# Values of the windowed attention layers projected once per token and carried through DRAM

## What is computed

```python
qkv = x @ Wqkv
q, k, v = jnp.split(qkv, 3, -1)
...
def look(t):
    p = jnp.pad(t, ((0, 0), (0, 0), (1, 0), (0, 0), (0, 0)))
    return jnp.concatenate([p[:, :, :nw], p[:, :, 1:]], axis=3)
bk2, bv2 = (look(bk), look(bv))
...
sim = jnp.einsum('bhwie,bhwje->bhwij', bq, bk2) * QK_SCALE
...
attn = jax.nn.softmax(sim, -1)
out = jnp.einsum('bhwij,bhwje->bhwie', attn, bv2)
```

## Time and profile before

| | us |
|---|---|
| median of 3 runs (7240.41 to 7246.15) | 7244.83 |
| the profiled execution | 7247.5 |
| its span | 7245.8 |
| the loop of the local layers, from 2273 to 6280 | 4007 |
| one iteration of it, of 95 alike | 42.11 |

### The profile page before, as it was taken

One profiled execution on the slowest core, in us unless ns is written; L12 is line 12 of the kernel. 1 busy time (PEld: TensorE's weight loads), 2 busy tenths in 40 slices (PEclk: granted clock), 3 DMA queues, 4 the chain that ended last, 5 costly groups with the idle time before them and its releaser, 6 DMA issues. The chain is left out here.

```text
span 7245.8 us, 217809 instructions
## 1 busy us (share of the span) xinstructions
PE 6522.4 (90%) x79314; PEld 4468.9 (62%) x79314; DVE 4927.7 (68%) x14182; ACT 4182.4 (58%) x10030; POOL 2901.3 (40%) x2911
## 2 busy tenths in 40 slices
PE   7999979999988888888888888888888888879998
PEld 5777657776655565555555556555555555557676
DVE  4555535555657777777777777777777777668378
ACT  4666637776224655656655665565665566446355
POOL 0000010000004666666666666666666666530030
PEclk9999989999989999999999999999999999979999
DMA  1000000000000000000000000000000000010210
GB/s 34 24 25 25 23 27 29 28 28 22 10 33 20 23 4 5 23 4 5 5 23 5 4 5 22 5 5 4 23 5 4 23 4 5 5 37 16 81 38 24
DMA packets 131939, 133.17 MB, mean 18 GB/s; under 512 B 40302, under 2 KB 121982, under 8 KB 130814
## 3 DMA queue, kind: packets, MB, share of 16 engines
q1 hardware_dynamic: 115454, 103.45, 4.4%
q0 software_dynamic: 7936, 24.28, 1.1%
q10 hardware_dynamic: 8448, 4.20, 0.2%
HBM read 55.48 MB, written 10.49 MB: 9 GB/s over the span
## 5 line engine op out<-in xcount | busy, mean ns | idle before, releaser
L937 POOL TENSOR_TENSOR l_rot<-l_rot,l_by_sin 128x512 f32<-128x512 f32 x768 | 961.1, 1272 | 438.6 <-DVE l_by_sin L1301 424.5
L944 POOL TENSOR_TENSOR l_rot<-l_rot,l_norms 128x512 f32<-128x512 f32 x768 | 793.7, 1064 | 485.0 <-DVE l_norms L1322 485.0
L1019 PE MATMUL bank<-w_w,l_x 128*128 (+1 forms) x1536 | 802.0, 631 | 133.8 <-DVE l_by_sin L1301 126.3
L1198 ACT ACTIVATE l_squares<-bank 128x512 f32<-128x512 f32 x768 | 447.5, 596 | 518.9 <-DVE l_square_sums L1306 491.8
L1025 PE MATMUL bank<-w_w,l_x_windows 128*128 (+1 forms) x1536 | 721.0, 602 | 0.0
L1297 DVE TENSOR_TENSOR l_rot<-bank,l_cos 128x512 f32<-128x512 f32 x768 | 519.2, 676 | 295.7 <-ACT l_squares L1198 294.4
L486 PE MATMUL bank<-a_qk 64*128 64x256 f32 (+2 forms) x2660 | 679.5, 381 | 6.1 <-DVE a_qk L668 3.5
L402 POOL DMA_DIRECT2D a_w<-in_a x23 | 13.0, 565 | 1554.2 <-PE bank L514 1431.0
L593 ACT ACTIVATE a_probs_t<-bank 128x512 f32<-128x512 f32 (+1 forms) x656 | 355.9, 554 | 353.7 <-PE bank L494 353.7
L1219 ACT ACTIVATE l_probs_t<-bank 128x512 f32<-128x512 f32 x384 | 208.7, 595 | 598.2 <-PE bank L1061 598.2
L1035 PE MATMUL bank<-ident,l_rot 128*128 128x128 f32 x3072 | 476.4, 283 | 74.3 <-ACT l_probs_t L1219 48.0
(11 more groups left out here) (265 smaller groups left out, 14415.8 us busy)
## 6 DMA issues: line engine op xcount, KB each, us to landing
a_x<-normed_t SPq DMA_DIRECT2D x320, 128.0 KB, 2.0
l_stage_rows<-inner SPq DMA_DIRECT2D x98, 128.0 KB, 2.1
w_w<-in_w SPq DMA_DIRECT2D x6, 2048.0 KB, 9.5
l_shifted_half<-inner SPq DMA_DIRECT2D x98, 63.5 KB
f_w<-in_f SPq DMA_DIRECT2D x9, 514.5 KB, 3.2
a_w<-in_a POOLq DMA_DIRECT2D x18, 256.0 KB, 2.9
f_w<-in_f POOLq DMA_DIRECT2D x9, 512.0 KB, 4.4
c_x<-normed_t SPq DMA_DIRECT2D x36, 128.0 KB, 2.0
```

The costliest lines, as they stand in the source:

```text
L937: nc.gpsimd.tensor_tensor(rot[s][n][:], rot[s][n][:], by_sin[n % 2][:], ALU.add).then_inc(summed, 1)
L944: nc.gpsimd.tensor_tensor(mine, mine, along(norms[s][:, 8 * n:8 * n + 8], HD), ALU.mult)\
L1019: nc.tensor.matmul(rows_p[i][:], x[:, W + i * P:W + (i + 1) * P], layer_w(layer, quad * QUAD, QUAD), start=True, stop=True).then_inc(rows_ ...
L1198: nc.scalar.activation(squares[i][:], rows_p[i][:], ACT.Square).then_inc(squared, 1)
```

## The change

The values are projected once per token. `project_v` multiplies the two tiles of 128 tokens of x by the same 512 columns of weights: two matmuls in a half in place of four. ACT moves both banks into `v_rows` [128, 2, 512], ahead of the first exponential. SP then stores `v_rows` (512 KB) to a DRAM buffer `values` of 288 rows by 512, one buffer for each o, whose first 32 rows are zero; and reads it back with four DMAs of 256 KB, each for 32 partitions of `v`, rows of 2 KB: 128 rows of the buffer from 0, 32, 128 and 160 on, so that each token lands both as "own" and as "before". `weigh` waits for these reads (`v_loaded`), the read waits until `weigh` of unit h is through with the old values (`heads_filled`), and ACT waits before it fills `v_rows` that the store before has landed (`v_stored`).

The values are now of unit h + 2 (before: h + 1), so they are projected in both halves behind `project_rows`, ahead of `output` in the first half. POOL's copy and `x_windows` are gone, and ACT no longer moves values between or behind the exponentials. `gates`, `output` and the transposes keep their places. The load of `w_f` at a layer's fourth iteration stands behind the store and the reads of the first half; scales and `w_w` behind those of the second.

```diff
-                def copy_window(f):
-                    pool.wait_ge(x_moved, f + 1)
...
                 def project_v(o, fill, layer):
-                    for j in range(4):
-                        reached(pe, t_freed[j % 2], fill + j // 2)
-                        nc.tensor.matmul(t_p[j % 2][:], x_windows[:, j].rearrange("p t s c -> p (t s c)"),
-                                         layer_w(layer, wv_at + o * QUAD, QUAD), start=True, stop=True)\
-                            .then_inc(t_filled[j % 2], 2)
+                    for i in range(2):
+                        reached(pe, t_freed[i], fill)
+                        nc.tensor.matmul(t_p[i][:], x[:, tile_of(i)], layer_w(layer, wv_at + o * QUAD, QUAD), start=True,
+                                         stop=True).then_inc(t_filled[i], 2)
...
+                def store_v(u, o, fill):
+                    for i in range(2):
+                        sp.wait_ge(t_freed[i], fill + 1)
+                        sp.sem_inc(begun, 1)
+                    sp.dma_start(v_dram[o][W:, :].rearrange("(i p) n -> p i n", p=P), v_rows[:]).then_inc(v_stored, DMA)
+
+                def load_v(u, o):
+                    sp.wait_ge(v_stored, (u + 1) * DMA)
+                    sp.sem_inc(begun, 1)
+                    for i in range(2):
+                        for s in range(2):
+                            at = i * P + s * W
+                            sp.dma_start(v[HD * i + W * s:HD * i + W * (s + 1), :, o * QUAD:(o + 1) * QUAD],
+                                         v_dram[o][at:at + P, :].rearrange("(j c) n -> c j n", c=W)).then_inc(v_loaded[o], DMA)
...
+                def send_v(g, o):
+
+                    h = 2 * g + o
+                    sp.wait_ge(v_loaded[o], (g + 1) * 4 * DMA)
+                    sp.sem_inc(begun, 1)
+                    store_v(h + 2, o, t_fill(h))
+                    sp.wait_ge(heads_filled, 4 * h + 4)
+                    sp.sem_inc(begun, 1)
+                    load_v(h + 2, o)
...
                     for e in range(2):
                         pe.wait_ge(t_freed[e], fill + 1)
                     pe.wait_ge(masked, 2 * h + 2)
+                    pe.wait_ge(v_loaded[o], ((h >> 1) + 1) * 4 * DMA)
...
+                def move_v(u, i, fill):
+                    act.wait_ge(t_filled[i], 2 * (fill + 1))
+                    if i == 0:
+                        reached(act, v_stored, u * DMA)
+                    nc.scalar.activation(v_rows[:, i, :], t_p[i][:], ACT.Copy).then_inc(t_freed[i], 1)
...
                         exps(h, 0)
-                        if more:
-                            move_v(1 - o, 2, fill)
                         exps(h, 1)
-                        if more:
-                            move_v(1 - o, 3, fill)
                         if o == 1 and not last:
                             move_x(g + 2, f_fill(g) + 1)
```

More of the change, by code:

```diff
@@ L816, in local_layers @@
         stage_rows = sb("stage_rows", [P, 2, D])
-        x, x_windows = sb("x", [P, W + SEQ]), sb("x_windows", [P, 4, 2, 2, W])
+        x, v_rows = sb("x", [P, SEQ]), sb("v_rows", [P, 2, QUAD])
+        v_dram = [nc.dram_tensor(f"{name}_values{o}", (W + SEQ, QUAD), F32, kind="Internal").ap() for o in range(2)]
         scales, tables = sb("scales", [P, 2, QUAD]), [sb(n, [P, 2, QUAD]) for n in ("cos", "sin")]
@@ L845, in t_fill @@
         def t_fill(h):
-            return 5 * h + 4
+            return 4 * h + 4 if not isinstance(h, int) or h <= 2 * LAST else 8 * LAST + 7
         def f_fill(g):
@@ L894, in iteration @@
                     stage_x(g + 2)
+                    if not last:
+                        send_v(g, 0)
                     sp.wait_ge(normed, g + 1)
@@ L899, in iteration @@
                     shift((g + NB - 1) & (NB - 1))
+                    if L is not None:
+                        sp.wait_ge(ffn_added, NB * L + 19)
+                        sp.sem_inc(begun, 1)
+                        sp.dma_start(fw[:], t["f2"][bass.ds(L + 1, 1), :, :].rearrange("a p n -> p (a n)"))\
+                            .then_inc(fw_loaded, DMA)
+                    if not last:
+                        send_v(g, 1)
+                def send_v(g, o):
[4 more added lines that the diff above has]
+                    sp.wait_ge(heads_filled, 4 * h + 4)
+                    sp.sem_inc(begun, 1)
+                    load_v(h + 2, o)
                 def load_layer(L):
-                    sp.wait_ge(ffn_added, NB * L + 19)
-                    sp.sem_inc(begun, 1)
-                    sp.dma_start(fw[:], t["f2"][bass.ds(L + 1, 1), :, :].rearrange("a p n -> p (a n)")).then_inc(fw_loaded, DMA)
                     sp.wait_ge(tables_ready, L + 1)
@@ L912, in load_layer, with layer @@
                         .then_inc(w_loaded, DMA)
+                def layer(L):
+                    with sp.Fori(0, 2) as m:
+                        iteration(NB * L + m)
+                    iteration(NB * L + 2, L)
+                    load_layer(L)
                 load_scales(0)
                 stage_x(0)
+                sp.wait_ge(cleared, 2)
+                for o in range(2):
+                    sp.dma_start(v_dram[o][0:W, :], heads_t[0:W, 0:2, :].rearrange("p a n -> p (a n)")).then_inc(v_cleared, DMA)
+                sp.wait_ge(v_cleared, 2 * DMA)
                 shift(NB - 2)
@@ L918, in _ @@
                 stage_x(1)
[L919 to L922, removed]
+                for u in range(2):
+                    store_v(u, u, u)
+                    load_v(u, u)
+                with sp.Fori(0, DEPTH - 1) as L:
+                    layer(L)
                     with sp.Fori(3, NB) as m:
                         iteration(NB * L + m)
+                layer(DEPTH - 1)
+                with sp.Fori(NB * (DEPTH - 1) + 3, LAST) as g:
+                    iteration(g)
+                iteration(LAST, last=True)
                 sp.wait_ge(normed, LAST + 2)
@@ L1144, in iteration @@
                         fill, more = t_fill(h), o == 0 or not last
-                        turned = fill + 2 if more else fill
+                        turned = fill if last else fill + 1
                         if not last:
@@ L1165, in iteration @@
                         if more:
-                            turn_qk(h + 1, 1 - o, fill + 3)
+                            turn_qk(h + 1, 1 - o, turned + 1)
                         if o == 0:
@@ L1248, in start @@
                     square(0, 1)
-                    for j in range(4):
-                        move_v(0, j, 0)
+                    for i in range(2):
+                        move_v(0, i, 0)
                     square(1, 0)
                     square(1, 1)
+                    for i in range(2):
+                        move_v(1, i, 1)
                     move_qk(0, 2)
```

53 lines of the change are left out of this document (18 added, 35 removed).

## The result

| | us |
|---|---|
| before, median of 15 runs (7237.98 to 7246.15) | 7242.86 |
| after, median of 15 runs (7242.49 to 7267.86) | 7256.37 |
| ratio, with its 95% interval | 1.0019 (1.0011 to 1.0027) |
| profiled execution of after, its span | 7253.68, 7252.0 |

The account below looks back on a forecast made before the run. Waits for DVE, not PE, were taken to pace most of the first half, and ACT's move of x `gates`. Terms -116 + 4 + 2 + 29 = -81 us gave 7164 us, range 7110 to 7250.

Parts of the forecast that it names:

- The chain: Waits through one loop iteration, with PE's work removed: 40.89 us against 42.11, 1.22 saved, 116 us over 95 iterations.
- the rival that PE is the bound: Waits for DVE close up and all 3.59 us an iteration arrive: 6904 us; whole or half gain 7%.
- only the first part of the gain comes: Second half's gain is eaten by an unseen wait; 0.74 us by 95 remains: 7210 us; 10%.
- the clock: Longer idle ahead of `gates` (3.11 us) lowers PE's clock in one iteration in five: 19 falls at 1.54 us, 29 us.
- The first rival: Clock falls in most iterations at the idle between `turn_x` and `gates`: up to 7281 us, slower; 14%.
- Layer boundaries: `w_f`, queued behind four reads on SP, reaches `gates` about 0.4 us late at five boundaries: 2 us, up to 15.
- Transfers: Two stores and eight reads more on SP in each iteration slow the engines by 0.04 us: 4 us.
- the rival of late transfers: A store taking over 20 us delays ACT's moves, exponentials and DVE; at 21 us, 7354 us; 6%.
- the idles of `turn_normed`: Sign on PE: `turn_normed` idles 1.1 us, ended by `normalise_rows`; `gates` idles about 3.1 us.
- the quiet `weigh`: Sign on PE: `weigh` waits for no DMA, the reads being issued some 38 us earlier.
- the undisturbed period: Sign in the loop: the period between two `stage_x` falls to 40.9 us, or 41.2 in the mean.
- the loop's clock: Sign in the loop: clock below 1.00 by a few hundredths; below 0.93, falls in most iterations are at work.

Follow-up runs that it names:

- the doses above: Kernel after with one or two matmuls on constants in PE's idle ahead of `gates`: 7205.58 and 7159.89 us; with four, 7152.96.
- no_transfers: Kernel after without the store of `v_rows`, the reads back into `v` and their waits (`v` is zeros): 7286.01 us, ratio 1.0065.
- fill_second: Kernel after plus four matmuls on constants (about 1.9 us) between `turn_x` and `gates` in every second half: 7152.96 us, ratio 0.9877.
- before_short: Kernel before, with second-half `project_v` matmuls on 320 of 512 columns, so a longer idle ahead of `gates`: 7305.49 us, ratio 1.0082.
- fill_first: Kernel after plus four matmuls on constants (1.9 us) in the first half, ahead of `output`: 7345.89 us, ratio 1.0144.
- wf_early: Kernel after with the load of `w_f` issued ahead of SP's four reads at a layer's fourth iteration: 7246.81 us, ratio 1.0008.

## Why the prediction was wrong

**The chain was right**, step by step: start to the end of `normalise_rows` 17.90 (18.00 forecast), to PE 0.14 (0.20), `turn_normed` to `weigh` 0.38 (0.31), to DVE's rotation 3.87 (3.87), to the second exponential 7.46 (7.46), to `gates` 1.39 (1.39), to the end 9.65 (9.66). Sum 40.79 against 40.89. That only a third of PE's 3.59 us arrives, and that the second half's 1.88 merely lengthen the idle, is what the trace shows; the rival that PE is the bound (6904) is out, and so is that only the first part of the gain comes.

**The term that failed is the clock.** The prediction named the place and the mechanism, and then chose one iteration in five, 19 falls at 1.54 us, 29 us. It was 57 of 93, and the falls away from the boundaries cost 2.0 us each (100 us for 51); with the boundaries' share some 112 us. Both factors were low: the step put at 29 us cost four times that. The count rested on two idles of the earlier trace rows, 2.39 with a fall and 2.57 without; the second stands in another stage, with other work around it. In this loop the doses above give the count that was missing: an idle of 2.3 cost 7 falls, one of 2.75 26, one of 3.19 51. Whether the other idles of the iteration (0.84 us at `ups`, 1.3 at `project_rows`) set that tolerance was not tested. Choosing near the low end because the rows show "idle alone deciding nothing" used the openness of the evidence as if it were evidence for few. The price rested on a single fall that hit `project_rows`, a group of 1.98 us; behind `gates` it hits four groups in a row, all on the chain.

The first rival had the right mechanism, and its break-even of 75% of the iterations at 1.54 us becomes 59% at the measured price (1.16 / 1.96, the 1.96 from 112 / 57). The real share, 57 of 93 or 61%, is just past it, so the gain and the loss nearly cancel. The rule cited from the Trainium skill, TensorE: Matmul & The Clock Gate, "HAM oscillation — how this bites in real kernels", that each wait costs the clock of the burst behind it, was nearer than my number, though 36 of the 93 iterations kept it. The section tells it of waits for DMA that are longer than the idle here, a condition that the prediction left out.

**Layer boundaries** were put at 2 us, 15 at most, and took 19 beside their clock. There are six and not five, and the 15 has no working: reads of 11.6 us, put into the sum beside it, would make `w_f` 9.2 us late at each. The order on SP was read rightly, the four reads were overpriced (1.73 for all, against 2.8), but the step kept the `shift` between the reads and `w_f` at its time of before: its second DMA held SP for 5.15 us in place of 2.59. It is the new transfers ahead of it that do this: the median over the loop is 2.63 before, 5.04 in after and 2.68 in no_transfers. `w_f` was issued 29.25 us after the iteration's start (3067.01 - 3037.76, where its `project_rows` begins), not 27.7. In fill_second a late `w_f` cost 5.1 us a boundary, since it cost a fall too.

**Transfers.** The 4 us were some 13: 0.14 an iteration, against 0.04 taken from the boundary of before. Both new waits stay hidden, as forecast; the store of 512 KB lands in 3.2 us and a read of 256 KB in 4.4, within the bounds given, and the rival of late transfers is out:

```profile
l_v<-l_values SPq DMA_DIRECT2D x768, 256.0 KB, 4.4
l_values<-l_v_rows SPq DMA_DIRECT2D x192, 512.0 KB, 3.2
```

**Of what was to be seen**, the idles of `turn_normed` (0.79, 1.1 forecast) and `gates`, the quiet `weigh` and the undisturbed period came true; the mean period was 42.2, not 41.2, and the loop's clock 0.96, not below the 0.93 that I had set for the first rival, though that rival was at work. That mark was set too low: the second of the four iterations above lost 1.7 us and still shows 0.96.

## What to carry to other kernels

When an edit takes work from PE in a stretch that ends in a wait for another engine, it doesn't shorten the stretch but lengthens the rest, and the rest can cost the clock of what follows it: read the gain from the chain of waits, and then price the new idle by what stands behind it on PE, not by a fall seen elsewhere. If the count of falls is unknown, a run with a little useless work in the idle tells what they cost, and may be the remedy as well. Real work freed from its wait, here by another PSUM bank for `turn_x`, shortens the chain, but in this kernel it kept the clock only together with the useless work (7142 us alone, 7126 with the useless work alone, 7084 with both). A DMA queued ahead of a rarely loaded weight costs nothing in the common iteration and several microseconds at each boundary; look at the whole queue, also at what stands between.

## What the runs showed of the hardware

- The clock fell at idles well under the 3.19 us of after. Of the 87 iterations that are no layer boundary it did so in 26 at 2.75 us (46 in before_short), in 7 at 2.3, in 43 at 1.4 us where shorter idles (0.28 and 0.34) and transposes followed, and in none at 1.45 where `gates` and all the transposes followed closely.
- Equal idles gave unequal counts: 51 in after, 80 in fill_first and 82 in no_transfers, of the same 87 and all at 3.19 us. The falls come in a pattern that repeats over several iterations (in after often one of 43.1 us, one of 42.4, then one or two of 40.8). What decides between them stays open: these kernels differ in the length of the iteration and in their transfers, and no run changed one of these alone.
- Leaving out transfers, or 1.3 us of work, made kernels slower (1.0065 against 1.0019, and 1.0082 against 1); adding 1.9 us of useless work made one faster.
- The second DMA of the `shift`, of 0.2 KB, held SP for 2.6 us in the kernel before, 5.15 behind four reads of 256 KB in after (the medians over the loop are 2.63 and 5.04, and 2.68 in no_transfers), and 8.30 behind `w_f` and four reads in wf_early.
